# Two masked graph-attention layers: the adjacency tile is loaded twice by GpSimd's DMA queue as bf16, once added onto a tile that holds the zero columns, and both masks become one bf16 pass each

## The reference

```python
h = x @ W                                             # layer 0
e = leaky_relu((h @ a_src)[:, None] + (h @ a_dst)[None, :], 0.2)
valid = (adj > 0) & (h.sum(axis=1) != 0)[None, :]
att = softmax(where(valid, e, -1e9), axis=1); att = where(valid, att, 0)
L = valid.sum(axis=1); top = att.max(axis=1)
attention = where(att >= 1e-4, att, 0) * L[:, None]
attention = where((top > 1e-4)[:, None], attention, 0)
x = layernorm(x + elu(h + attention @ h))

s = leaky_relu(x @ ks.T, 0.2)                         # layer 1
s = where(adj > 0, s, -9e15)
x = layernorm(x + softmax(s, axis=1) @ ks)
```

## Time and profile before

| | us |
|---|---|
| median of three runs | 931.74 |
| the profiled execution | 931.15 |
| its span | 929.4 |
| TensorE busy | 890.7 |
| ScalarE busy | 772.6 |
| VectorE busy | 758.8 |
| GpSimd busy | 52.0 |

### The profile page before, as it was taken

How to read it: one execution, slowest core, us unless ns; L and a number is a source line. 1 busy time by engine, 2 the same in 40 slices (tenths; PEclk the granted TensorE clock), 3 DMA queues, 4 the chain that set the end, 5 groups by cost and what they waited for, 6 DMA issues and landing times.

```text
span 929.4 us, 17647 instructions
## 1 busy us (share of the span) xinstructions
PE 890.7 (96%) x7111; PEld 789.7 (85%) x7111; DVE 758.8 (82%) x1252; ACT 772.6 (83%) x787; POOL 52.0 (6%) x136
## 2 busy tenths in 40 slices
PE   7764999999999999999999999999999999999997
PEld 5653899888888998888889988888899888888986
DVE  3978788898888888988888889888888898888433
ACT  3564888899888888998888888988888889888764
POOL 0000000000000000000000000000000000000000
PEclk9986999999999999999999999999999999999999
DMA  9122222112222221122222211222222112220000
GB/s 290 80 91 94 94 97 94 52 57 89 97 98 97 97 94 54 53 92 97 98 97 95 97 51 50 97 98 97 97 95 97 47 55 97 97 97 6 2 7 6
DMA packets 19537, 76.70 MB, mean 83 GB/s; under 512 B 1920, under 2 KB 14336, under 8 KB 15360
## 3 DMA queue, kind: packets, MB, share of 16 engines
q1 hardware_dynamic: 19456, 75.57, 23.2%
HBM read 73.47 MB, written 2.10 MB: 81 GB/s over the span
## 4 chain that ended last, share of the span: by engine, by line
PE 93%; DVE 3%; issue 1%; ACT 1%; DMA 1%; SPq 0%; POOL 0%; POOLq 0%; DVEq 0%; ACTq 0%
PE work L232 25%; PE bank L331 25%; PE bank L350 24%; PE work L308 6%; PE work L313 6%; PE work L309 6%; PE work L248 1%; PE work L249 1%; DVE att L584 1%; DMA att<-x 1%; DVE att L556 0%; ACT att L425 0%; PE bank L356 0%; PE work L260 0%; DVE adj_sb L551 0%
## 5 line engine op out<-in xcount | busy, mean ns | idle before, releaser
L232 PE MATMUL work<-ident,att 128*128 128x128 f32 x2080 | 246.1, 278 | 23.9 <-ACT att L455 13.1
L232 PEld LDWEIGHTS work<-ident,att 128*128 128x128 f32 x2080 | 236.8, 143 | 31.1 <-issue 22.4
L350 PE MATMUL bank<-k_all,att1T 128*128 128x128 f32 x2048 | 237.5, 275 | 0.0
L331 PE MATMUL bank<-h_all,att0T 128*128 128x128 f32 x2048 | 234.3, 275 | 0.0
L350 PEld LDWEIGHTS bank<-k_all,att1T 128*128 128x128 f32 x2048 | 233.9, 192 | 0.1
L331 PEld LDWEIGHTS bank<-h_all,att0T 128*128 128x128 f32 x2048 | 231.7, 192 | 0.0
L638 DVE CUSTOM_DVE_ANT_0 att<-att,mask 128x1024 f32<-128x1024 f32 x128 | 156.7, 1225 | 28.2 <-ACT att L455 22.4
L455 ACT ACTIVATE att<-work 128x1024 f32<-128x1024 f32 x128 | 131.1, 1025 | 32.3 <-PE work L313 32.3
L467 ACT COPY att1T<-work 128x1024 f32<-128x1024 f32 x128 | 126.0, 1012 | 30.1 <-PE work L232 30.1
L584 DVE SCALAR_TENSOR_TENSOR att<-att,cut 128x2048 f32<-128x2048 f32 x64 | 147.4, 2344 | 0.0
L556 DVE CUSTOM_DVE_ANT_0 att<-adj_sb,d_all 128x4096 f32<-128x4096 bf16 x31 | 137.2, 4425 | 1.1
(11 more groups left out here) (85 smaller groups left out, 428.1 us busy)
## 6 DMA issues: line engine op xcount, KB each, us to landing
adj_sb<-adj SPq DMA_DIRECT2D x32, 2048.0 KB, 8.4
att<-x SPq DMA_DIRECT2D x4, 512.0 KB, 6.0
x_sb<-x SPq DMA_DIRECT2D x32, 64.0 KB, 7.4
out<-x SPq DMA_DIRECT2D x32, 64.0 KB, 1.5
w_sb<-W SPq DMA_DIRECT2D x1, 64.0 KB, 3.9
a_sb<-a SPq DMA_DIRECT2D x2, 0.5 KB, 3.8
k_all<-ks SPq DMA_DIRECT2D x1, 0.5 KB, 15.6
```

Source lines behind the costliest of these rows:

```text
L232: mm = pe.transpose(work[:, n % SLOTS, b * P:(b + 1) * P], source(c * PER + b), ident[:, :])
L331: mm = pe.matmul(acc0, att0T[:, k * P:(k + 1) * P], h_all[:, k, :], start=(k == 0), stop=(k == BLOCKS - 1))
L350: mm = pe.matmul(acc1, att1T[:, k * P:(k + 1) * P], k_all[:, k, :], start=(k == 0), stop=(k == BLOCKS - 1))
```

## The change

`adj_sb` becomes a bf16 tile, and a second bf16 tile, `valid_sb`, is added. All adjacency loads go to GpSimd's queue, since only there can a DMA convert or add.

- `load_adj(f)` loads adjacency tile f into `adj_sb`, converted from int32 to bf16. It waits for `mask_built` of the tile before. `build_mask` now reads bf16.
- SyncE copies `zero_cols` (0, or -NO_EDGE in a zero column) into `valid_sb` by a DMA from SBUF to SBUF, where it loaded the adjacency before, and behind the same semaphore `masked0`.
- `add_adj(f)` waits for that copy, loads tile f a second time and adds it onto `valid_sb`, in descriptors of at most 8192 bytes.
- `mask0(f)` waits for this sum and makes the mask of layer 0 with one one-input pass (is it <= 0, times -NO_EDGE) over `valid_sb`, in place, instead of the minimum of two tiles.

```diff
-        adj_sb = sb("adj_sb", [P, N], I32)
+        adj_sb = sb("adj_sb", [P, N], BF16)
+
+        valid_sb = sb("valid_sb", [P, N], BF16)
...
-        mask_and_zero = adj_sb[:, 0:HALF].bitcast(BF16)
...
+        zeros_laid, valid_in = sem("zeros_laid"), sem("valid_in")
...
-            sp.dma_start(adj_sb[:, :], adj_rows[0]).then_inc(adj_in, 16)
             sp.dma_start(k_all[:, :, :], ks.rearrange("(b p) d -> p b d", p=P)).then_inc(kall_in, 16)
             sp.dma_start(x_sb[0][:, :], x_rows[0]).then_inc(x_in[0], 16)
             sp.dma_start(x_sb[1][:, :], x_rows[1]).then_inc(x_in[1], 16)
-            sp.wait_ge(mask_built, 1)
-            sp.dma_start(adj_sb[:, :], adj_rows[1]).then_inc(adj_in, 16)
+            sp.wait_ge(zero_found, D_CHUNKS)
+            sp.dma_start(valid_sb[:, :], zero_cols[:, :]).then_inc(zeros_laid, 16)
             sp.wait_ge(masked0, 2)
-            sp.dma_start(adj_sb[:, :], adj_rows[2]).then_inc(adj_in, 16)
+            sp.dma_start(valid_sb[:, :], zero_cols[:, :]).then_inc(zeros_laid, 16)
 
             def slot(t):
                 if t + 3 < TILES:
                     sp.wait_ge(masked0, t + 3)
-                    sp.dma_start(adj_sb[:, :], adj_rows[t + 3]).then_inc(adj_in, 16)
+                    sp.dma_start(valid_sb[:, :], zero_cols[:, :]).then_inc(zeros_laid, 16)
...
             def mask0(f):
                 p = f % 2
-                dve.wait_ge(mask_built, f + 1)
-                nc.vector.tensor_tensor(mask_and_zero, mask[f % MASKS][:, :], zero_cols[:, :],
-                                        ALU.min).then_inc(zero_masked, 1)
+                dve.wait_ge(valid_in, 16 * f)
+                nc.vector.tensor_scalar(valid_sb[:, :], valid_sb[:, :], 0.0, -NO_EDGE, ALU.is_le,
+                                        ALU.mult).then_inc(zero_masked, 1)
                 dve.wait_ge(zero_masked, f)
                 if f >= 2:
                     dve.wait_ge(turned0, 4 * (f - 2) + 4)
-                nc.vector.tensor_tensor_reduce(att0[p][:, :], mask_and_zero, d_all[:, :], 1.0, -NO_ROW_MAX,
+                nc.vector.tensor_tensor_reduce(att0[p][:, :], valid_sb[:, :], d_all[:, :], 1.0, -NO_ROW_MAX,
                                                ALU.add, ALU.max, top0[p][:, :]).then_inc(masked0, 1)
...
-            for t in range(TILES + 2):
+            def load_adj(f):
+                if f > 0:
+                    pool.wait_ge(mask_built, f)
+                nc.gpsimd.dma_start(adj_sb[:, :], adj_rows[f]).then_inc(adj_in, 16)
+
+            def add_adj(f):
+                pool.wait_ge(zeros_laid, 16 * f)
+                nc.gpsimd.dma_start(valid_sb[:, :], adj_rows[f], accum_op=ALU.add, max_dma_last_dim=8192).then_inc(valid_in, 16)
+
+            load_adj(0)
+            load_adj(1)
+            add_adj(1)
+            load_adj(2)
+            add_adj(2)
+            deviation0(0)
+            load_adj(3)
+            add_adj(3)
+            for t in range(1, TILES + 2):
+                if t + 3 < TILES:
+                    load_adj(t + 3)
                 if t >= 2:
                     deviation1(t - 2)
                 if t < TILES:
                     deviation0(t)
+                if t + 3 < TILES:
+                    add_adj(t + 3)
```

## The result

The changed kernel takes 942.15 us (median of 4 runs, 941.28 to 943.40); the kernel before, on the same chip, 931.35. The ratio is 1.0117 with an interval from 1.0098 to 1.0135: 10.8 us slower. The profiled executions are 943.4 and 931.15 us, their spans 941.5 and 929.4. The sign was forecast. The time lies in the wide range of the prediction (928.5 to 1000 us), but just above the 933 to 941 us that it gives as the forecast's own, and the loss is three times the +3.2 us of the sum. So the question is where 12.1 us of span come from when 3.2 were expected.

The account below looks back on a forecast made before the run. The prediction took TensorE, busy in all of each slot, to bound the kernel. Its terms -2.3 + 3.5 + 2.0 = +3.2 us gave 934.4 us, forecast as a 934.9 us median, own range 933 to 941, wide range 928.5 to 1000.

Parts of the forecast that it names:

- the +3.2 us of the sum: Whole kernel: -2.3 for masks, +3.5 at the start and +2.0 in slot 1, added to the profiled 931.15 us.
- Masks, -2.3: Tile 2's two mask passes, in TensorE's 13.1 us wait: each 1.14 us shorter, together -2.3 us.
- Start, +3.5: Start: tile 0's early load delays x's last piece by 5.1 us, less 1.5 us of cover: +3.5 us.
- Ring in a slot, 17.8 us against 21.0 of room, cost 0: Every slot: zero-column copy, GpSimd's issue and adding load take 17.8 us, within 21.0 us of room, so nothing waits.
- Slot 1, +2.0: Slot 1: tile 2's maximum ends late, so tile 3's sum and x1 come late; TensorE waits 2.0 us more, once.
- `deviation0(0)` delayed, hidden: GpSimd's list: tile 2's sum stands ahead, making x1 1 to 2 us later, hidden with some 4 us of cover.
- The ring longer than the slot (1062 us): L551 of every slot waits for the adding load if converting and adding halve the rate: 1062 us, chance 0.20.
- GpSimd held by the `cut`: Slots: VectorE's cut of 4.61 us delays GpSimd's issue of the sum: about +46, 977 us; chance 0.07.
- That the mask passes hold GpSimd: At `load_adj`: by the skill's rule VectorE's two 1.15 us passes lock GpSimd out, moving the sum 1.2 us at most.
- Faster (929.4): Tile 2's masks: x is not held up and the copy-to-sum chain takes at most 16 us, leaving only -2.3; chance 0.19.

Follow-up runs that it names:

- The early load in the kernel before: The kernel before, with adjacency tile 0's plain int32 load issued at the program's start from ScalarE's queue: 936.46 us, ratio 1.0067.
- the mended start: The changed kernel, with GpSimd loading adjacency tile 0 once x's second piece is in and SyncE loading the keys after tile 0: 936.47 us, ratio 1.0047.
- tile 3's edit: The changed kernel, with tile 3's layer-0 mask made by the minimum of mask and zero columns, without its copy and adding load: 935.46 us, ratio 1.0056.
- The longer ring: The changed kernel, with SyncE copying the zero columns three times in each slot, one after the other: 1097.05 us, one run.
- The repaired kernel: The changed kernel, with tile 0's load after x's second piece, keys after tile 0, and tile 3's layer-0 mask by the minimum: 929.82 us, ratio 0.9984.
- the one converted load: The changed kernel, with tile 0 loaded after x's second piece, keys after it, no copy or adding load, minimum kept: 930.49 us, ratio 0.9994.

## Why the forecast was right in sign and three times too small

- **Masks, -2.3.** Right. L545 and L551 take 1227 and 1218 ns at the median; 1150 were in the sum and 1.2 us was the other value given. And the wait at tile 2 brought TensorE from +7.2 back to +5.0, which is -2.2 (then another -0.4, as the turn behind the shorter wait ran 4.96 us instead of 5.35, which is the clock and not the masks). That the long wait became 9.3 us and not the 10.8 forecast is TensorE's own lateness, as said above. In the slots they bring nothing, as said.
- **Start, +3.5: measured +6.5.** This step failed. It looked only at x's *last* piece, and gave it 1.5 us of cover. The second piece has none: TensorE waited 0.72 us for it already before. The last has 0.4 us, as it lands at 11.6 and is turned from 12.0 on. And the delay is 6.2 us for each of the last three pieces, not 5.1. So the term was 5.1 less 1.5 where 6.2 less 0 was due; the last 0.3 are four small matmuls (L283) that ran longer. TensorE's last turns of x end at 20.0 us, where the prediction had about 17. The early load in the kernel before (+6.2) and the mended start (-6.5) show from both sides that the place makes it, each to within 1.5 us.
- **Behind the start, +0.7.** Not forecast. The second group of L260 takes 5.01 us instead of 3.39, with a granted clock of 0.72 from 40 to 46 us, and the turn behind it is 0.9 shorter than before. Where the slow stretch falls differs between kernels: with tile 3's edit, which leaves the start as it is, L260 takes 3.39 us and the turn 6.29. What sets it was not tried.
- **Ring in a slot, 17.8 us against 21.0 of room, cost 0.** The conclusion is right, the size 1.5 us too high: 16.3. The copy takes 4.9 us up to GpSimd's issue instead of 5.8, and the sum lands 11.3 us after the start of its issue, against 12.0 for issue and load together. The longer ring shows what happens above the room, not where it ends.
- **Slot 1, +2.0: measured +6.4.** The mechanism is right, the place and the cause also (tile 3's edit gives back 5.7), the size is not. From L551 to x1 it is 9.1 us, as reckoned. Of the difference of 4.4, 2.3 are the wait. For 1.7 of them, the ring is 19.5 us there instead of 17.8: copy 7.1 us from its issue to GpSimd's, then 12.3 to the landing of the sum, of which 0.7 is the issue of 1.93 us, beside L545. For 0.6, TensorE gets there sooner after tile 2's maximum (24.3 us instead of 24.9), since the turn and the sums behind the long wait are shorter. The other 2.2 are matmuls at a lower clock behind the wait, for which the sum had no term.
- **End, +1.1.** Not forecast; from the last output DMA's issue to the end of the span it is 2.8 us instead of 1.7. That DMA itself lands in 1.5 us in both, so the time lies behind its landing (1.6 us against 0.6). The cause was not found, below.
- **`deviation0(0)` delayed, hidden.** Right: x1 comes at 68.36, 2.0 us more than the general +7.2 behind its 59.16, and ScalarE's cast and TensorE's scores stand at +7.2.
- **Rivals.** The ring longer than the slot (1062 us): refuted, VectorE waits for it once. GpSimd held by the `cut`: refuted. At 407.77 L827 takes 1.26 us and is done before the `cut` starts at 410.07, and at 116.05 it takes 1.25 us, fully beside the `cut` of 115.68. That the mask passes hold GpSimd did come, and cost at the one place where it counted, in slot 1. Faster (929.4): it did not come. The repaired kernel, whose two edits take off what this rival leaves out, has 929.82 us; that the two numbers are so close is partly luck, as its trace adds up otherwise.

The new costs as they turned out: -2.6 + 6.5 + 0.7 + 6.4 + 1.1 = +12.1, the difference of the spans.

## What to carry to other kernels

A load that is given to another queue at the start of a kernel is not free because its queue is: look at what the first consumer waits for, piece by piece, the small DMAs too, and if the DMA engines are already full put the load behind those pieces by a semaphore and ahead of what nobody needs yet. Check a new chain of waits not only in the steady slot but in the first slots, where its producer runs late and its DMAs crowd; and price a wait of TensorE at more than its length, since the matmuls behind it may run at a lower clock (here 2.2 us on 4.3). Work taken off an engine is worth only the part of it that someone waits for: 67 us of VectorE's time were worth 2.2.

## What the runs showed of the hardware

- **A load that converts int32 to bf16** lands within 0.4 us of a plain one of the same source (8.6 or 8.8 us against 8.4), and GpSimd issues it in 0.59 us.
- **An adding load** lands 2.5 us later. The Trainium skill (Collectives: The Full Stack, "The bandwidth ceiling: the fold count and why AG ≠ RS ≠ AR") says of the add in a reduce-scatter that it costs by its two source reads. By the 411 GB/s of the earlier trace rows, reading another 1.05 MB is 2.55 us (an estimate): the trace agrees.
- **GpSimd's descriptor writing and VectorE's fast passes hold each other up.** The load issued at 53.30 us took 1.55 us, where the median is 0.587, beside L551 (53.51 to 54.73); and the other way round L545 at 93.55 took 1.46 us beside an issue of 1.93, where both are else 1.23 and 1.26.

```profile
53.30 1.55 POOL L823 DMA_DIRECT2D adj_sb<-adj  x1 [11.69 <-DVE mask L545]
...
93.55 1.46 DVE L545 TENSOR_SCALAR mask<-adj_sb 128x4096 bf16<-128x4096 bf16 x1
```

  The Trainium skill (SBUF — State Buffer, "SBUF: two separate sides") has GpSimd locked out during such passes; these rows agree (each long issue ends 0.1 us behind the pass beside it), and show that VectorE pays too, 0.23 us here. Beside the `cut`, a pass over two fp32 inputs, the issue is not longer.
- **The outputs land later in every kernel with the adding load**: 3.9 to 4.6 us at the median, 1.5 in the four without it, 2.1 where the load does not add. They share no queue with it. How it reaches them was not found.
- **The end of the kernel is longer where GpSimd issues loads.** The last output lands in 1.5 or 1.6 us in every kernel. From there to the end of the span it is 0.5 or 0.6 us in the three kernels in which GpSimd issues no DMA, 1.0 with the one converted load, 1.5 to 1.7 with the adding loads, and 3.6 where the second load does not add. So it does not follow how late the outputs land, and its cause was not found.
